# Fusion block on one core: the engines' hardware loops written out, with every wait on a constant

## What is computed

```python
h = tok(x)                        # 5 shifted copies of a 518x518x3 image, 16x16 patches, LayerNorm, dense: 1024 tokens x 128
h = concat([h, txt], axis=1)      # + 77 text tokens = 1101
h = h + causal_attn(layernorm(h)) # 8 heads of 64, 1101 x 1101 scores, causal mask, softmax
h = h + sparse_attn(layernorm(h)) # 8 heads of 16; each row keeps its 16 largest logits, softmax over them
```

## Time and profile before

| | us |
|---|---|
| median of three executions | 5894.83 |
| lowest, highest | 5883.47, 5908.94 |
| span of the profiled execution | 5921.3 |
| busy: PE / DVE / POOL / ACT | 4872.7 / 4044.9 / 3189.5 / 2745.0 |
| mean granted TensorE clock, share of full | 0.855 |

### The profile page before, as it was taken

How to read it: one execution, slowest core, us unless ns; L and a number is a source line. 1 busy time by engine, 2 the same in 40 slices (tenths; PEclk the granted TensorE clock), 3 DMA queues, 4 the chain that set the end, 5 groups by cost and what they waited for, 6 DMA issues and landing times. The chain is left out here.

```text
span 5921.3 us, 104393 instructions
## 1 busy us (share of the span) xinstructions
PE 4872.7 (82%) x33480; PEld 3298.2 (56%) x33928; DVE 4044.9 (68%) x6958; ACT 2745.0 (46%) x5521; POOL 3189.5 (54%) x1495
## 2 busy tenths in 40 slices
PE   5999699887988688886998879886988879884777
PEld 3666565555555555564555645555555555553444
DVE  1111487766888488775778578884878668883887
ACT  1222255544555355553555445552555435552444
POOL 1000176653766176663666357661767447762887
PEclk8555798998999899898889989997999989996666
DMA  3020301003020300103020120203010030003000
GB/s 49 2 28 0 47 3 29 3 5 48 3 30 2 51 2 9 24 5 48 2 30 2 28 26 3 30 2 52 3 22 9 5 48 3 3 2 48 1 0 4
DMA packets 221648, 104.95 MB, mean 18 GB/s; under 512 B 183616, under 2 KB 198544, under 8 KB 221072
## 3 DMA queue, kind: packets, MB, share of 16 engines
q1 hardware_dynamic: 221072, 97.68, 11.1%
HBM read 78.98 MB, written 18.67 MB: 16 GB/s over the span
## 5 line engine op out<-in xcount | busy, mean ns | idle before, releaser
L510 POOL TENSOR_SCALAR A<-A 128x1101 f32<-128x1101 f32 x576 | 1732.6, 3008 | 1652.8 <-DVE A L1125 1651.6
L839 ACT COPY PT<-causal_ps 128x512 f32<-128x512 f32 (+3 forms) x1984 | 1064.8, 561 | 1216.9 <-PE causal_ps L600 1213.3
L515 POOL TENSOR_TENSOR A<-A,E 128x1101 f32<-128x1101 f32 x576 | 1378.8, 2394 | 101.6 <-POOL A L510 98.3
L1100 DVE MAX8 top<-logit_ps 128x8 f32<-128x1101 f32 x576 | 753.9, 1309 | 546.6 <-PE logit_ps L620 544.2
L600 PE MATMUL causal_ps<-ident,A 128*128 128x128 f32 (+1 forms) x5184 | 926.6, 313 | 18.2 <-POOL A L515 17.7
L727 PE MATMUL out_ps<-qk,PT 128*128 128x64 f32 x5760 | 875.7, 300 | 24.4 <-ACT PT L839 24.0
L672 PE MATMUL causal_ps<-qk 64*128 64x512 f32 (+3 forms) x1792 | 864.7, 596 | 11.7 <-ACT PB L903 6.6
L727 PEld LDWEIGHTS out_ps<-qk,PT 128*128 128x128 f32 x5760 | 808.7, 215 | 81.9 <-ACT PT L839 35.4
L1120 DVE MAX8 top<-A 128x8 f32<-128x1101 f32 x576 | 753.4, 1308 | 83.8
L600 PEld LDWEIGHTS causal_ps<-ident,A 128*128 128x128 f32 (+1 forms) x5184 | 693.2, 162 | 206.9 <-issue 148.7
L701 PE MATMUL out_ps<-PT,Vh 128*32 128x128 f32 (+1 forms) x10368 | 763.0, 302 | 38.8 <-DVE O L1088 14.9
(11 more groups left out here) (140 smaller groups left out, 3931.3 us busy)
## 6 DMA issues: line engine op xcount, KB each, us to landing
stack<-qk_parts SPq DMA_DIRECT2D x128, 288.0 KB, 20.2
X<-in_x SPq DMA_DIRECT2D x248, 121.5 KB, 4.1
qk_parts<-O SPq DMA_DIRECT2D x16, 864.0 KB, 4.8
Wp<-in_L_attn_W_in SPq DMA_DIRECT2D x96, 64.0 KB, 2.0
out<-OUTB SPq DMA_DIRECT2D x8, 512.0 KB
stack<-in_L_tok_conv_w SPq DMA_DIRECT2D x30, 64.0 KB, 2.4
X<-in_x SPq DMA_DIRECT2D x8, 108.0 KB
H<-in_txt SPq DMA_DIRECT2D x8, 38.5 KB
```

The lines of the kernel that those rows point to most:

```text
L510: nc.gpsimd.tensor_scalar(A[:, k % 3, :], A[:, k % 3, :], NEG, None, ALU.is_equal).then_inc(marked, 1)
L515: nc.gpsimd.tensor_tensor(A[:, k % 3, :], A[:, k % 3, :], E1[:, k % 2, 0:L], ALU.mult).then_inc(chosen, 1)
L839: last = nc.scalar.copy(PT[:, slot, 128 * q0:128 * (q0 + full)], bank[:, 0:128 * full])
L1100: nc.vector.max(top[:, s, 0:8], logit_ps[:, 0:L]).then_inc(top8, 1)
```

## The change

Every `Fori` becomes a Python `for` over the same range, so `c` and `p` are plain numbers, each wait compares with a constant, each address is fixed, and no jump is left but those at the start and end of a block. `hold` loses its bump and so is a plain wait, which the next instruction can carry. The order of the instructions that do work, their shapes and the buffers stay. The diff, with the loops of ACT and DVE, which change exactly as those of PE, cut:

```diff
@@ -340,7 +340,6 @@
         def hold(eng, s, value, counter):
 
             eng.wait_ge(s, value)
-            eng.sem_inc(counter, 1)
@@ -418,7 +417,7 @@
                 sp.dma_start(H[0:TXT, NT - 1, :], txt[c]).then_inc(txt_loaded, 16)
-                with sp.Fori(0, NP) as p:
+                for p in range(0, NP):
@@ -439,7 +438,7 @@
             load_images(0, first=True)
             cycle(0, True, False)
-            with sp.Fori(1, B - 1) as c:
+            for c in range(1, B - 1):
                 cycle(c, False, False)
@@ -497,7 +496,7 @@
                 pool.sem_inc(held_g, 1)
-                with pool.Fori(0, NP) as p:
+                for p in range(0, NP):
                     for k in range(STEPS):
@@ -516,7 +515,7 @@
             halos(0)
-            with pool.Fori(1, B) as c:
+            for c in range(1, B):
                 halos(c)
                 weights(c)
             weights(B)
@@ -784,22 +783,22 @@
             tokens(0)
             a_round(0, 0, False, True, False)
-            with pe.Fori(1, NP) as p:
+            for p in range(1, NP):
                 a_round(0, p, False, True, True)
             a_round(0, NP, False, True, True)
             projections(0, True)
-            with pe.Fori(1, B) as c:
+            for c in range(1, B):
                 tokens(c)
                 sparse_inputs(c)
                 a_round(c, 0, True, True, False)
-                with pe.Fori(1, NP) as p:
+                for p in range(1, NP):
                     a_round(c, p, True, True, True)
                 a_round(c, NP, True, True, True)
                 output(c)
                 projections(c, False)
             sparse_inputs(B)
             a_round(B, 0, True, False, False)
-            with pe.Fori(1, NP) as p:
+            for p in range(1, NP):
                 a_round(B, p, True, False, True)
             a_round(B, NP, True, False, True)
             output(B)
...
```

More of the change, by code:

```diff
@@ L934, in _ @@
             a_round(0, 0, False, True, False)
-            with act.Fori(1, NP) as p:
+            for p in range(1, NP):
                 a_round(0, p, False, True, True)
@@ L938, in _ @@
             projections(0)
-            with act.Fori(1, B) as c:
+            for c in range(1, B):
                 tokens(c)
                 a_round(c, 0, True, True, False)
-                with act.Fori(1, NP) as p:
+                for p in range(1, NP):
                     a_round(c, p, True, True, True)
@@ L1177, in _ @@
             a_round(0, 0, False, True, False)
-            with dve.Fori(1, NP) as p:
+            for p in range(1, NP):
                 a_round(0, p, False, True, True)
@@ L1181, in _ @@
             projections(0)
-            with dve.Fori(1, B) as c:
+            for c in range(1, B):
                 tokens(c)
                 a_round(c, 0, True, True, False)
-                with dve.Fori(1, NP) as p:
+                for p in range(1, NP):
                     a_round(c, p, True, True, True)
```

## The result

Four executions of the changed kernel took 5712.81 to 5748.12 us, median **5742.83**; four of the kernel before on the same chip 5883.47 to 5908.94, median 5893.46. The ratio is 0.9728, with a 95% interval of 0.9676 to 0.978: 2.7% faster, 151 us, where 125 were forecast. The profiled execution of the changed kernel spans 5746.3 us, that of the kernel before 5921.3, so the two traces differ by 175; some 24 us of that is only that the old trace is of an execution slower than its median.

The account below looks back on a forecast made before the run. PE was taken to bound somewhat over half of the steps and DVE the others; 73 + 7 + 30 + 11 + 4 = 125 us off the 5894.8 us median gave 5770 us, range 5690 to 5830.

Parts of the forecast that it names:

- part 4: Waits and register work ahead of DVE's instructions: closing these gaps saves 30 us in mixed rounds and 11 us in cycle 8.
- part 2: PE's outer loop, last projection to next item's first causal projection: six jumps back at 1.16 us, 7 us saved.
- Part 1: PE's inner loop, cycles 1 to 7: 14 crossings fall from 24.09 to 18.84 us without the jump, 73 us saved.
- Part 3: Cycles 0 and 8: taken branches cost under 1 us and register work is covered in cycle 0, so nothing saved.
- a cap of 5 us: Clean mixed round: PE's work and waits for ACT fill 110 of 115 us, so DVE's savings give at most 5 us.
- Rival A: Only the jumps pay; DVE's gaps close into a longer wait for PE: 80 us saved, 5815 us, chance 0.20.
- The floor from POOL: Cycle 8: POOL's L510, L515 and the 0.17 us between need 5.57 us a step, limiting DVE's 5.81 us step.
- Part 5: Granted clock in steps 1 to 17 of a round: no change, 0 us, with bounds taken from the rivals.
- Rival B: The clock stays up in mixed rounds: 2.8 us less in each of 28, 78 us more saved, 5692 us, chance 0.18.
- Rival C: Mixed rounds: dips of the clock come in all rounds, losing 322 us less 125, so 6092 us, chance 0.09.
- rival D: PE's written-out instruction stream starves: stalls of 2.9 us at only 45 places would cancel the gain, chance 0.03.
- Part 6: Handoffs through ACT, POOL and SP: some 40 uncovered `hold` waits at 0.11 us, 4 us saved.

Follow-up runs that it names:

- the run with two transfers: Changed kernel with PE held at the 14 former inner-loop jump places by two small ACT-issued transfers, one behind the other; 5866.42 us, ratio 0.9955.
- join moved: Changed kernel with PE's join (L708) of a sparse tile placed behind the second group of causal transposes, in PE's order only; 5604.92 us, ratio 0.9498.
- step 2 filled: Changed kernel with 16 extra small matmuls in step 2 of each mixed round, without effect on the output; 5700.89 us, ratio 0.9663.
- both: Changed kernel with PE's join behind the second group of causal transposes and 16 extra matmuls in step 2 of each mixed round; 5602.87 us, ratio 0.9517.

## Why the prediction was right, and where it wasn't

The forecast of 5770 us had the direction, the two main mechanisms and the range; it was 27 us too high. The term that was mis-sized is part 4: 41 us were put down for it, and in the traces it is some 86. One term came out by luck, part 2.

**Part 1, 73 us: right, 72.7.** The trace of before held both kinds of crossing, and the new code was the kind it already showed. The lower end (41 us, idleness alone) would have been wrong, since the clock's share belongs to the idleness: the run with two transfers shows that. The text named 18.2 to 18.8 us as the sign; it is 18.9, since the row was 18.84 and nothing in a crossing was DVE's to win.

**Part 2, 7 us: not borne out.** 452.21 us of the earlier trace rows became 442.05, 10 us less, which is near the number but not for its reason. The first window, which never had a jump, fell by 1.55 us (63.61 to 62.06); the other six fell by 1.44 each (64.77 to 63.33). And the 1.16 us by which the six were longer, read as the price of a jump, is still there without one (63.33 - 62.06 = 1.27). The sums also scatter: 439 to 446 us in the kernels without an outer jump on PE, 434 to 452 in those with one. So no run shows that the six outer jumps cost anything.

**Part 3, nothing: right** (2.3 us up to the first MAX8).

**Part 4, mixed rounds, 30 us: the term that was mis-sized.** The gaps closed as it said (L1120's idle 83.8 to 19.7, predicted 17; L1088's "issue" 78.4 to 1.1, predicted 10). What they are worth was then set at 1.1 us a round, under a cap of 5 us that PE's 110 of 115 us left. A clean stretch won 2.4 us: in 28 rounds 67, next to the upper end of 69 that the text had worked out itself and set aside. The cap wasn't reached, and nothing in the rows argued for so small a part of it. `hold` was priced as a whole, wait and bump together; the bump put back alone brings all of the 0.11 us back.

The Trainium skill (VectorE: DVE Perf Modes, the section on the DRAIN) says that a semaphore after each of eight copies costs nothing extra. The kernel after agrees where the semaphore rides on the operation: L1115 raises one and L1119 waits for it, and starts 0.034 us after it. A bump that is an instruction of its own between them makes this 0.148 us (85.3 / 576), and that case the section doesn't speak of.

Rival A, by which DVE's gaps only turn into longer waits for PE, was right in part: DVE's wait for the logits grew from 544.2 to 600.0 us, while some 150 us of gaps closed.

**Part 4, cycle 8, 11 us: 18.7.** The floor from POOL was wrong. The shortest steps take 5.44 us, such as the one that ends with the L1099 at 5402.89, with DVE working without a gap; that is below the 5.57 that POOL was said to need. The mean of L515 hides two lengths:

```profile
5396.78 3.00 POOL L509 TENSOR_SCALAR A<-A 128x1101 f32<-128x1101 f32 x1 [0.77 <-DVE A L1124]
5399.93 2.52 POOL L514 TENSOR_TENSOR A<-A,E 128x1101 f32<-128x1101 f32 x1
5403.07 3.00 POOL L509 TENSOR_SCALAR A<-A 128x1101 f32<-128x1101 f32 x1 [0.62 <-DVE A L1124]
5406.22 2.13 POOL L514 TENSOR_TENSOR A<-A,E 128x1101 f32<-128x1101 f32 x1
```

POOL is a step behind DVE with buffers between, and in the longer steps between, where DVE waits for logits, it catches up: in the first and third row POOL waits for DVE before L509. So single steps go below its mean. And the gap between L509 and L514, said to stay at 0.17 us, fell to 0.15 (5399.93 - 5396.78 - 3.00). With the bumps put back it is 0.17 again, so that was POOL's bump.

**Part 5, the clock, 0: right on balance, and not understood.** Of the 58 us of steps 1 to 17, clean stretches give 21 x 2.39 = 50; the dips take 2476.7 - 21 x 112.76 = 109 us after and 2534.7 - 21 x 115.15 = 117 before. The text said that dips follow the thin early steps; that holds for where they start, but what makes one long or short is not shown. Rival B (half of the dips or more gone) was the case in four kernels of this study (bumps put back, join moved, step 2 filled, both), by edits that the change doesn't hold. Rival C didn't come, rival D neither: PE's waits on "issue" in the rounds are 0.2 us at most (the first row; the second, between cycles, is the one place with more):

```profile
PE logit_ps L619 <- issue: 16.3, 84, 0.2
...
PE causal_ps L539 <- issue: 10.5, 7, 1.5
```

**Part 6, 4 us:** not told apart from the rest.

The sum of the parts as measured in the traces is 72.7 (crossings) + 58.0 + 20.7 (steps of rounds 1 to 3, and of rounds 0) + 18.7 (cycle 8) + 3.4 + 2.3 (between cycles, and the start) - 0.9 (elsewhere) = 175 us, against the 151 between the medians.

**Still open:** what makes a dip 3.4, 13.7 or 34.1 us long, and why the kernel with bumps has seven of 13.7 us in its 28 rounds where the one without has seven of 34.1. There is one trace of each, but the clocks of all executions of the two lie apart (0.875 to 0.882 against 0.866 to 0.873). The two were measured in different sets, and never side by side. A run with the bumps left in DVE alone and no other wasn't tried.

## What to carry to other kernels

Price a loop's jump from two crossings of the same trace, one fallen into and one jumped back, and over a stretch long enough to hold what follows: here some 3 us of idleness was 5.2 us of time. Where PE is the engine that bounds the steps, look at its own short waits first: moving one instruction group behind another (the join) took 138 us, about as much as all loops of five engines written out, though half of that came by the clock and wasn't foreseen. Before an edit is credited with a change of the clock, look whether it changed the step where the clock falls. And where rounds come in a few lengths, count the clean ones and the long ones apart before a difference of under 1% is put down to an edit.

## What the runs showed of the hardware

- A jump back whose branch takes 3.48 us in the median costs no more, to some 0.2 us, than idleness without a jump: 24.1 us a crossing with 3.0 us of idleness, 25.3 with 3.6 and no jump, and 18.9 with neither.
- At these crossings PE idle for 1.27 us kept its clock in 12 of 12 places; idle for 2.1 us it lost it in 2 of 2, idle for 3.3 to 4.8 us in 14 of 14, and idle for 2.6 to 3.4 us at a jump in 14 of 14.
- Dips that start at step 2 mostly last 3.4, 13.7, 34.1 or 44.4 us, and the same instructions in the next round may have none.
- A semaphore bump as an instruction of its own between two dependent DVE operations costs 0.11 us (0.145 against 0.034 us between L1116 and L1120); the register work ahead of L1088 cost about as much again per tile (78.4 + 10.9 us in 576).
- One POOL multiplication of 128 x 1101 float32 values takes 2.13 us on every third tile and 2.52 us on the others, in the order of the three buffers of `A`.
- Taking idle time out of more engines doesn't add up: all loops but PE's written out gain 14 us in the median where DVE's alone gain 55, at a lower mean granted clock (0.850 against 0.862 in the median).
